# The last attention of a four-layer block: scores with queries in partitions, and scores turned, with keys in partitions

## The reference, cut to what matters

```python
def _L3_xattn_ref(x, latents, ...):          # x: (2, 64, 256) context, latents: (2, 1024, 256)
    H, Dh = (8, 64)
    scale = Dh ** (-0.5)
    xn = layer_norm(x, ln_media_w, ln_media_b)
    zn = layer_norm(latents, ln_lat_w, ln_lat_b)
    q = (zn @ Wq) ...                        # (2, 8, 1024, 64)
    kv_in = jnp.concatenate([xn, zn], axis=1)   # 64 + 1024 keys
    k = (kv_in @ Wk) ...
    v = (kv_in @ Wv) ...
    sim = jnp.einsum('bhqd,bhfd->bhqf', q * scale, k)
    alphas = jax.nn.softmax(sim, axis=-1)
    out = jnp.einsum('bhqf,bhfd->bhqd', alphas, v)
    return out.transpose(0, 2, 1, 3).reshape(b, Nz, H * Dh) @ Wout
```

## Time and profile before

| what | value |
|---|---|
| median of the runs (lowest, highest) | 2316.48 us (2310.39, 2322.75) |
| the profiled execution | 2309.96 us |
| its span, first to last instruction | 2308.1 us |
| mean granted TensorE clock | 0.884 |
| busy share of the span: PE, PEld, DVE, ACT, POOL | 80%, 57%, 58%, 46%, 25% |
| the chain that ended last, by engine | PE 63%, DVE 13%, POOL 8%, ACT 7%, issue 6% |

### The profile page before, as it was taken

The page is one execution under the profiler, slowest core; times in us unless marked ns, Lnnn a source line. Parts: engine busy times, 40 slices in busy tenths (PEclk is TensorE's granted clock), DMA queues, the critical chain, the costliest instruction groups (busy, mean ns, idle before and its releaser), DMA issues.

```text
span 2308.1 us, 30551 instructions
## 1 busy us (share of the span) xinstructions
PE 1838.9 (80%) x10608; PEld 1320.3 (57%) x10608; DVE 1345.6 (58%) x2559; ACT 1052.7 (46%) x2069; POOL 574.3 (25%) x816
## 2 busy tenths in 40 slices
PE   6743999818875788884997687899999999986895
PEld 3243899805653322262554355688888888873553
DVE  5842544364768467741112688688888888843334
ACT  3112443203236777731221354678876777730440
POOL 2133000072457444432001555101001000105014
PEclk9756999959977799985999897899999999988997
DMA  9112322120000000051112000000000000022343
GB/s 368 46 62 74 115 94 95 43 68 1 1 18 1 1 1 1 1 219 47 37 37 81 28 1 1 1 1 1 1 1 1 1 1 1 1 101 73 99 135 91
DMA packets 60099, 112.53 MB, mean 49 GB/s; under 512 B 7829, under 2 KB 51288, under 8 KB 57520
## 3 DMA queue, kind: packets, MB, share of 16 engines
q1 hardware_dynamic: 52272, 90.02, 11.0%
q0 software_dynamic: 7680, 20.57, 2.8%
HBM read 71.12 MB, written 39.80 MB: 48 GB/s over the span
## 4 chain that ended last, share of the span: by engine, by line
PE 63%; DVE 13%; POOL 8%; ACT 7%; issue 6%; DMA 2%; another core or an unknown queue 2%; SPq 0%; POOLq 0%; DVEq 0%; ACTq 0%
PE psum L203 54%; PE psum L1997 4%; POOL arena L1579 2%; POOL arena L781 2%; ACT arena L1378 2%; POOL xb L776 1%; PE psum L237 1%; DVE arena L218 1%; DVE arena L518 1%; DVE arena L208 1%; DVE arena L1460 1%; ACT arena L2059 1%; DVE rounded L2081 1%; POOL arena L214 1%
## 5 line engine op out<-in xcount | busy, mean ns | idle before, releaser
L203 PE MATMUL psum<-arena 128*128 128x256 f32 (+17 forms) x4423 | 1032.4, 445 | 183.6 <-DVE arena L1494 30.6
L203 PEld LDWEIGHTS psum<-arena 128*128 128x128 f32 (+5 forms) x4423 | 556.8, 177 | 576.5 <-issue 346.9
L203 PE MATMUL psum<-rounded 128*128 128x256 f32 (+5 forms) x3648 | 557.3, 307 | 20.1 <-DVE rounded L817 19.6
L203 PEld LDWEIGHTS psum<-rounded 128*128 128x128 f32 (+2 forms) x3648 | 492.1, 188 | 58.0 <-issue 17.8
L2081 DVE SCALAR_TENSOR_TENSOR rounded<-psum,rounded 128x512 fp32r<-128x512 f32 (+4 forms) x456 | 255.7, 586 | 93.0 <-ACT rounded L2067 43.5
L2067 ACT ACTIVATE rounded<-psum 128x512 fp32r<-128x512 f32 (+1 forms) x320 | 164.9, 554 | 35.5 <-PE psum L2001 18.6
L781 POOL DMA_INDIRECT arena<-yb,arena x80 | 78.4, 981 | 406.4 <-DMA yb<-arena 361.2
L1378 ACT ACTIVATE arena<-psum,arena 128x1024 f32<-128x1024 f32 (+1 forms) x192 | 156.6, 911 | 48.9 <-PE psum L203 48.9
L2107 DVE TENSOR_REDUCE arena<-psum 128x1 f32<-128x1024 f32 x128 | 155.6, 1216 | 1.0 <-PE psum L203 1.0
L1997 PE MATMUL psum<-arena 128*128 128x128 f32 x1024 | 141.1, 278 | 13.3 <-ACT arena L2062 9.5
L2059 ACT ACTIVATE arena<-psum,arena 128x1024 f32<-128x1024 f32 x128 | 143.7, 1123 | 1.7 <-DVE arena L2109 1.7
(11 more groups left out here) (249 smaller groups left out, 2074.9 us busy)
## 6 DMA issues: line engine op xcount, KB each, us to landing
arena<-in_w SPq DMA_DIRECT2D x8, 2048.0 KB, 7.9
yb<-arena SPq DMA_DIRECT2D x102, 128.0 KB
xb<-arena SPq DMA_DIRECT2D x5, 2048.0 KB, 17.6
arena<-xb SPq DMA_DIRECT2D x70, 128.0 KB, 2.2
arena<-in_w1u SPq DMA_DIRECT2D x4, 2048.0 KB, 14.7
arena<-xb SPq DMA_DIRECT2D x8, 512.0 KB
arena<-in_w1d SPq DMA_DIRECT2D x1, 4096.0 KB, 13.5
arena<-in_w3b SPq DMA_DIRECT2D x1, 4096.0 KB, 16.9
```

Of the source, the lines that this page charges most:

```text
L203: return e.matmul(o, l, r, start=start, stop=stop, skip_group_check=True)
```

## The change

The last attention is laid out anew. The unit of work is now a block G of one pair of heads and 512 queries (16 blocks), cut into nine steps j: eight tiles of 128 keys and one of the 64 context keys. In each step:

- `pe_scores3` makes scores with keys in PSUM's partitions and queries in the columns, in float32. The two heads of the pair lie in the upper and the lower 64 rows of TensorE (the first two products of the step), and each writes a bank of its own. Two more products with a single row each, of fp32r operands, add the negated maximum of each query to the scores.
- `act_weigh3` takes the exponential of both heads at once; nothing is turned afterwards, since keys already lie in partitions.
- `pe_values3` takes the weights as they are, in float32, two steps later; the two heads write the upper and the lower 64 partitions of one bank (64 columns of TensorE each).
- `pe_rough3` and `dve_rough3` find the maxima of the next block: one rounded product of rounded queries and keys, with queries in partitions, of which only the maximum is used.
- `pool_sum3` adds up the weights over the key tiles on POOL; a product with ones (side step s) sums them over the partitions and spreads the sums, and `dve_divide3` takes reciprocals of 512 columns in four pieces and multiplies.
- `side3` says which extra step ends a slot: the sums (s), the queries two blocks ahead (q), keys and values of the next pair (k, v), the output projection of two row tiles (o), and the turning of the next block's maxima (m), for which `x3_NM` is turned by a product with the identity. They share one bank, and each waits until the one before it has been read out.

The transposes, the split into high and low parts, the context's own scores and the turning back of the output are gone. SyncE now loads the next layer's weights at the stage's start. The line numbers of the new kernel differ (its `mm` is line 149).

```diff
+        def side3(G, j):
+
+            n = G // 2
+            if j == 1 and G:
+                return ("s", G - 1, 0)
+            if j == 2 and G + 2 < 16:
+                return ("q", G + 2, 0)
+            if 3 <= j <= 5 and n + 1 < 8:
+                return ("v" if G % 2 else "k", n + 1, j - 3)
+            if 6 <= j <= 7 and G >= 7 and (G - 1) // 2 % 4 == 3:
+                return ("o", G - 1, j - 6)
+            if j == 8 and G + 1 < 16:
+                return ("m", G + 1, 0)
+            return None
+
...
+        def pe_side3(e, s):
+            kind, a, c = s
+            i, bk = SIDE3_AT[s], side_bank3(s)
+            if i >= 8:
+                was = SIDE3[i - 1]
...
+            elif kind == "m":
+                e.wait_ge(s_mx, 48 + a + 1)
+                for t in range(4):
+                    m = mm(e, psum[0:65, bk, 128 * t:128 * t + 128], x3_NM[:, t, :], ident, True, True)
+            elif kind == "s":
+                e.wait_ge(s_pa, 8 * a + 8)
...
+        def pe_rough3(e, G, i):
+            n, bk = G // 2, rough3(G, i)
+            if i == 0:
+                e.wait_ge(s_kr, max(SIDE3_ROUNDED["q", G, 0], SIDE3_ROUNDED["k", n, 2]))
+            if G:
+                e.wait_ge(s_ar, 2 * (9 * G + i))
+            elif i >= 2:
+                e.wait_ge(s_ar, 2 * i - 2)
+            for a in range(2):
+                r = slice(64 * a, 64 * a + 64)
+                if i == 0:
+                    for t in range(4):
+                        m = mm(e, psum[:, bk[a], 64 * t:64 * t + 64], x3_QR[r, G % 3, 128 * t:128 * t + 128],
+                               x3_KR[r, n % 2, 1024:1088], True, True)
                 else:
+                    t, c = (i - 1) // 2, (i - 1) % 2
+                    m = mm(e, psum[:, bk[a], :], x3_QR[r, G % 3, 128 * t:128 * t + 128],
+                           x3_KR[r, n % 2, 512 * c:512 * c + 512], True, True)
+                m.then_inc(s_am, 1)
...
+        def dve_maxima3(e, G):
+            e.wait_ge(s_ar, 18 * G + 18)
+            settle(e, dve, e.tensor_reduce(x3_M1, x3_MX, AX.X, ALU.max))
+            e.tensor_scalar(x3_NM[:, :, 0:65:64], x3_M1, -1.0, None, ALU.mult).then_inc(s_mx, 1)
+
+        def pe_scores3(e, G, j):
+            n, g, rows = G // 2, 9 * G + j, 128 if j < 8 else 64
+            if g >= 2:
+                e.wait_ge(s_ex, 48 + g - 1)
+            for a in range(2):
+                r = slice(64 * a, 64 * a + 64)
+                mm(e, psum[0:rows, 2 * (g % 2) + a, :], x3_KF[r, n % 2, 128 * j:128 * j + rows], x3_QF[r, G % 3, :], True, False)
+            if j == 0:
+                e.wait_ge(s_mo, SIDE3_KEPT["m", G, 0])
+            for a in range(2):
+                m = mm(e, psum[0:rows, 2 * (g % 2) + a, :], x3_ONE[64 * a:64 * a + 1, 0:rows], x3_MR[64 * a:64 * a + 1, :],
+                       False, True)
+            m.then_inc(s_sc, 1)
+
+        def pe_values3(e, G, j):
+            n, g, rows = G // 2, 9 * G + j, 128 if j < 8 else 64
+            e.wait_ge(s_ex, 48 + g + 1)
+            if j == 0 and G:
+                e.wait_ge(s_oc, G)
+            for a in range(2):
+                m = mm(e, psum[64 * a:64 * a + 64, 4, :], x3_VF[0:rows, n % 2, j, 64 * a:64 * a + 64], x3_P[0:rows, g % 4, a, :],
+                       j == 0, j == 8)
+            m.then_inc(s_pv, 1)
+
+        def act_weigh3(e, G, j):
+            g, rows = 9 * G + j, 128 if j < 8 else 64
+            e.wait_ge(s_sc, 48 + g + 1)
+            if g >= 4:
+                e.wait_ge(s_pv, 40 + g - 3)
+                e.wait_ge(s_pa, 8 * ((g - 4) // 9) + max((g - 4) % 9, 1))
+            bk = 2 * (g % 2)
+            e.activation(x3_P[0:rows, g % 4].rearrange("p a n -> p (a n)"),
+                         psum[0:rows, bk:bk + 2, :].rearrange("p a n -> p (a n)"), ACT.Exp, scale=0.125).then_inc(s_ex, 1)
...
+        def dve_divide3(e, G, i):
+
+            b, p, h = block3(G)
+            if i == 0:
+                e.wait_ge(s_mo, SIDE3_KEPT["s", G, 0])
+            m = e.reciprocal(x3_RC[:, 128 * i:128 * i + 128], x3_SM[:, 128 * i:128 * i + 128])
+            if i == 3:
+                settle(e, dve, m)
+                e.wait_ge(s_oc, G + 1)
+                ov = x3_OE[:, p, 512 * h:512 * h + 512]
+                e.tensor_tensor(ov, ov, x3_RC, ALU.mult).then_inc(s_on, 1)
+
+        def pool_sum3(e, G, j):
+            g, rows = 9 * G + j, 128 if j < 8 else 64
+            ac = x3_AC[0:rows, G % 2]
+            e.wait_ge(s_ex, 48 + g + 1)
+            if j == 1:
+                if G >= 2:
+                    e.wait_ge(s_mi, SIDE3_AT["s", G - 2, 0] + 1)
+                m = e.tensor_tensor(ac, x3_P[:, (g - 1) % 4], x3_P[:, g % 4], ALU.add)
+            else:
+                e.wait_ge(s_pa, 8 * G + j - 1)
+                m = e.tensor_tensor(ac, ac, x3_P[0:rows, g % 4], ALU.add)
+            m.then_inc(s_pa, 1)
 
         def sp_xattn3(e):
...
             e.wait_ge(s_xt, 57)
-            for step in steps3():
-                pe_step3(e, step)
+            for s in FIRST3[:8]:
+                pe_side3(e, s)
+            e.wait_ge(s_mo, SIDE3_KEPT[FIRST3[7]])
+            for i in range(9):
+                pe_rough3(e, 0, i)
+            pe_side3(e, FIRST3[8])
+            for G in range(16):
+                for j in range(9):
+                    pe_scores3(e, G, j)
+                    if G + 1 < 16:
+                        pe_rough3(e, G + 1, j)
+                    if j >= 2:
+                        pe_values3(e, G, j - 2)
+                    elif G:
+                        pe_values3(e, G - 1, j + 7)
+                    if side3(G, j):
+                        pe_side3(e, side3(G, j))
+            pe_values3(e, 15, 7)
+            pe_values3(e, 15, 8)
+            for s in SIDE3[-3:]:
+                pe_side3(e, s)
 
```

493 lines of the change are left out of this document (157 added, 336 removed).

## The result

| kernel | median, us | lowest to highest | runs | clock |
|---|---|---|---|---|
| before, same chip | 2313.43 | 2308.58 to 2322.75 | 4 | 0.884 |
| changed | 2388.78 | 2380.73 to 2390.68 | 4 | 0.863 |

The change makes the kernel slower: ratio 1.031, with a 95% interval of 1.0286 to 1.0334. The forecast had the sign (slower, +34 us) but less than half of the size: 2389 us lies outside its range of 2292 to 2380. The profiled execution of the changed kernel took 2387.03 us, 77.1 more than the profiled one before (2309.96 us).

What follows compares the result with a forecast made beforehand. TensorE was taken to bound the stage. Slots 428, extra steps 142 and waits 16 gave a loop of 586 us (+9); with start +17 and end +8, +34 on 2309.96 us: 2344, range 2292 to 2380.

Steps and rivals of the forecast that it cites:

- The bound: Attention stage's loop: TensorE's instructions set the time, busy 560.3 of 577.5 us before; DVE 476, ACT 436 us.
- The slot: Each of 144 loop steps: scores, single-row products, rough scores, values and four shape changes take 2.98 us of TensorE.
- The change's shape price: TensorE, each change of tile shape: 0.09 us, and 0.11 or 0.05 on top for the first weight load.
- Rival A: Slots: changes between 64 rows and one row cost nothing, each slot loses 0.4 us, 2287 us; chance 0.12.
- rival C: Slots: 64-row pairs don't overlap, 2.2 us more in each of 144, 2661 us; chance 0.04.
- The wait for the maxima: Block ends: TensorE waits 1.1 us a block for DVE's maxima (bounds 0 and 2), 16 in all.
- The clock: Loop: TensorE's granted clock was 1.00 before and was taken to stay there.
- rival B: Loop: each block's wait for the maxima drops the clock to 0.94, 36 us more, 2380 us; chance 0.12.
- The sum: Whole kernel: loop +9, start +17, end +8, together +34 on 2309.96 us, 2344 us.
- the extra steps: Loop, at slot ends: queries 27, keys and values 62, maxima 16, sums 15, outputs 22, together 142 us.
- The start: Before the loop's first scores: 30 us instead of 13.0, +17, bounds 14 to 20 more.
- the end: From the last value step to the last statistics: one chain of 22.6 us instead of 14.9, +8.

Runs made afterwards that it cites:

- e4: Changed kernel with the single-row products made over 64 rows, zeros in the other 63 rows of the maxima; 2314.2 us, ratio 1.001 to before.
- e8: e6 with the steps of every other slot in reversed order, so that two slots' values stand side by side; 2284.5 us, ratio 0.987 to before.
- e7: Changed kernel with the second head of a pair taking queries and keys from the first head's 64 rows, timing only; 2757.9 us, ratio 1.1906.
- e1: Changed kernel with the negated maxima from one tensor_reduce, without DVE's small multiplication; 2338.7 us, ratio 1.009 to before.
- e2: Changed kernel with POOL's last addition of a block waiting until the next block's maxima are ready; 2343.1 us, ratio 1.0113 to before.
- e3: Changed kernel with ten unread TensorE products of 128 columns ahead of the wait for the maxima in 15 blocks; 2361.9 us, ratio 1.0192.
- e5: Changed kernel with the next block's rough scores ahead of the scores in each slot; 2325.5 us, ratio 1.0026 to before.
- e9: e6 with DVE's casts of the keys and queries moved behind the next slot's maxima; 2285.5 us, ratio 0.985 to before.
- e6: Changed kernel with the edits of e1, e4 and e5 together; 2282.3 us, ratio 0.9847 to before.

## Why the prediction was wrong

**The bound.** Right: TensorE bounds the loop before and after, and DVE's and ACT's relief by 189 and 233 us brought nothing.

**The slot.** Right: 2.94 us against 2.98, and each term within 0.1 when its change of shape is counted with it. The change's shape price, taken from the trace of before, is what e4 and e8 measured (0.2 and 0.17 us a change). Rival A is out (0.43 us between rough and single-row products, as with a change each), and so is rival C (e7, for the rows; for the columns the 1.01 us in which both heads' two passes of values fit).

**The wait for the maxima, the step that failed.** It had two of DVE's long maxima and "two small ones", 0.5 us, 1.1 us after the values' cover, with bounds 0 and 2. The cover and the long ones were right. One of the small ones took 1.50 us: it stood until POOL's addition was done. I had added durations of DVE instructions as if each were a property of DVE, and had set POOL's additions beside it as cover with only a count of their own (16 us a block). No term asked what the two do to each other. Worth: 35.3 us of waits instead of 16, so +17 in 15 blocks of the loop. e1 and e2, the same kernel without the overlap, have 12.1 and 15.4.

**The clock.** I kept it at 1.00 and gave rival B, a fall through this wait, a chance of 0.12 with the argument that the wait is half as long as the one in the earlier trace rows. That argument rested on the 1.1. With 2.2 us B's condition was met, and it came: 27 us (36 in B's sum, with a fall in every block instead of six). e3 shows the cause. So the two terms were not independent, and I had treated them as if they were: the wait's bound of 2 us should have carried B with it, +14 and +36 together, which gives 2394 (with the 27 that B turned out to cost, 2385), and the range should have reached that far.

**The sum.** Loop 586 + 17 (wait) + 27 (clock) - 6 (slots of 2.94) = 624, against 625 measured. That this meets to one microsecond is luck: the sum has no term for the half clock with which the loop begins (about 6 us), and the extra steps and the other small terms were together priced about 5 us too high, which I haven't taken apart further. The start, 27.6 against 30, lay within its bounds, and the end, 20.1 against 22.6, was 2.5 us too dear. The 7.2 us of a later start of the stage are in no term; between these kernels it lies anywhere in 11 us. e1, nearly the kernel that I had priced, measured 2338.7 where the forecast was 2344, and there too errors cancel: its loop was 11 us shorter than my 586 and its stage began 9 us later than before.

## What to carry to other kernels

When work is handed to POOL beside DVE, look for each short cast or multiplication on DVE with its operands in SBUF that stands in a chain: here its price was its own or the rest of POOL's instruction. Make it a reduce, move it to ACT, or let POOL wait. A wait of TensorE is priced with what it does to the clock, as one term with both ends, not as two chances. And count changes of the tile's shape: rows filled with zeros that avoid a change cost less than the change, here 47 us in all.

## What the runs showed of the hardware that I had not expected

- A DVE multiplication of 8 numbers in SBUF took 1.50 us beside a POOL addition that was already running, 0.17 us without it, and ended 0.03 us behind the addition whenever it had begun (1.90, 1.70, 1.50 and 0.51 us long in e5, e4, the changed kernel and e5 again); a cast 2.59 against 0.36 to 0.43 (e9), a multiplication of two tensors 2.38 against 0.69 (e6). In the changed kernel's loop maxima of 512 columns (0.66 to 0.69) and reciprocals of 128 (0.89 to 0.95) took the same with and without an addition beside them. The other way round the addition took 2.90 instead of 2.35 (e9).
- TensorE's clock fell from 2.4 to 1.2 GHz for 10.2 us at the end of waits of 2.2 us, at six waits of fifteen, and not once when needless products filled them (e3) or when they were 0.68 or 0.88 us long (e1, e2). With other work around waits of 2.4 us it fell at or within 1.6 us behind five of fifteen, for 3.4 us each (e4).
- With both products of a pair in the same rows, waits of 2.0 us were followed by half clock for 27 us and more, and once the clock fell after 20 us without a gap (e7).
- 64-row float32 pairs run side by side: the two passes of both heads' scores took 1.06 us with their change of shape, and 0.86 more in the same rows (e7).
